# Attention inside a decoder layer: the chain that makes the shift rows two places later on VectorE and ScalarE, the rows' DMAs six places behind the group's last product

## What is computed

```python
q = (x @ Wq.T + bq).reshape(B, N, HEADS, HEAD_DIM).transpose(0, 2, 1, 3)
k = (context @ Wk.T + bk).reshape(B, M, HEADS, HEAD_DIM).transpose(0, 2, 1, 3)
v = (context @ Wv.T + bv).reshape(B, M, HEADS, HEAD_DIM).transpose(0, 2, 1, 3)
attn = jax.nn.softmax(jnp.einsum('bhnd,bhmd->bhnm', q, k) * scale, axis=-1)
out = jnp.einsum('bhnm,bhmd->bhnd', attn, v)
```

## Time and profile before

| what | value |
| --- | --- |
| median of 3 runs | 1926.51 us (1926.38 to 1927.36) |
| the profiled execution, its own time | 1935.45 us |
| its span in the trace | 1933.5 us |
| mean granted clock of TensorE | 0.971 |
| PE busy | 1824.7 us, 94% |
| DVE busy | 1430.8 us, 74% |
| ACT busy | 1251.9 us, 65% |
| POOL busy | 445.2 us, 23% |

### The profile page before, as it was taken

One profiled execution on the slowest core, in us unless ns is written; L12 is line 12 of the kernel. 1 busy time (PEld: TensorE's weight loads), 2 busy tenths in 40 slices (PEclk: granted clock), 3 DMA queues, 4 the chain that ended last, 5 costly groups with the idle time before them and its releaser, 6 DMA issues. The chain is left out here.

```text
span 1933.5 us, 38723 instructions
## 1 busy us (share of the span) xinstructions
PE 1824.7 (94%) x12524; PEld 1288.2 (67%) x12524; DVE 1430.8 (74%) x3030; ACT 1251.9 (65%) x3128; POOL 445.2 (23%) x629
## 2 busy tenths in 40 slices
PE   7899999999999999789999999989999999899988
PEld 5677777777777777564666666656666663588853
DVE  8988888888888888647686868667777775566348
ACT  5646464646464645348989898878888886266614
POOL 1312121212121212421222121222232222100006
PEclk9999999999999999898999999989999996799999
DMA  7122131313131313433334343334343423721266
GB/s 235 53 55 96 50 101 49 102 48 103 50 102 48 103 47 104 137 97 93 105 90 122 91 117 102 111 106 116 100 121 92 125 68 103 228 92 47 75 210 257
DMA packets 123884, 200.60 MB, mean 104 GB/s; under 512 B 27184, under 2 KB 48688, under 8 KB 123440
## 3 DMA queue, kind: packets, MB, share of 16 engines
q1 hardware_dynamic: 114480, 179.20, 30.1%
q0 software_dynamic: 9216, 18.89, 3.9%
HBM read 117.27 MB, written 29.88 MB: 76 GB/s over the span
## 5 line engine op out<-in xcount | busy, mean ns | idle before, releaser
L1961 ACT ACTIVATE a_shared<-a_shared,a_mx 128x512 f32<-128x512 f32 x512 | 344.4, 676 | 57.7 <-DVE a_mx L2024 57.5
L2024 DVE TENSOR_REDUCE a_mx<-a_shared 128x1 f32<-128x512 f32 x512 | 328.3, 682 | 37.9 <-PE a_shared L2171 36.2
L1954 ACT ACTIVATE a_probs<-a_scores 128x512 f32<-128x512 f32 x512 | 302.8, 607 | 58.8 <-PE a_scores L2182 58.6
L2171 PE MATMUL a_shared<-a_ks,a_qs 96*128 96x512 f32 x512 | 213.7, 438 | 13.8 <-ACT a_shared L1961 8.5
L2182 PE MATMUL a_scores<-a_qs,a_ks 98*128 98x512 f32 x512 | 211.3, 427 | 9.8 <-DMA a_qs<-a_shift_rows 5.2
L2143 PE MATMUL a_shared<-link 128*128 128x512 f32 x768 | 201.7, 399 | 9.7 <-DVE a_v L2018 7.4
L1086 PE MATMUL m_proj<-m_xt_hi,link 128*128 128x512 f32 x448 | 182.2, 407 | 3.9 <-DVE m_acc L780 3.5
L2171 PEld LDWEIGHTS a_shared<-a_ks,a_qs 96*128 96x128 f32 x512 | 96.2, 194 | 132.9 <-ACT a_shared L1961 59.5
L600 ACT ACTIVATE m_xw<-m_added,m_wdt 128x64 f32<-128x64 f32 x256 | 55.8, 329 | 192.7 <-DVE m_xdt L868 192.7
L2143 PEld LDWEIGHTS a_shared<-link 128*128 128x128 f32 x768 | 146.6, 192 | 47.3 <-DVE a_v L2018 10.9
L1087 PE MATMUL m_proj<-m_xt_lo,link 128*128 128x512 f32 x448 | 176.5, 394 | 0.0
(11 more groups left out here) (305 smaller groups left out, 3828.2 us busy)
## 6 DMA issues: line engine op xcount, KB each, us to landing
m_dec<-step_decay SPq DMA_DIRECT2D x64, 256.0 KB, 4.1
a_qs<-link SPq DMA_DIRECT2D x256, 64.0 KB, 2.0
m_ce<-run_decay SPq DMA_DIRECT2D x128, 112.0 KB, 3.1
a_ks<-a_k_hi POOLq DMA_DIRECT2D x192, 64.0 KB, 2.4
e_x<-x SPq DMA_DIRECT2D x11, 1024.0 KB, 5.6
m_xt_in<-x_t_in SPq DMA_DIRECT2D x8, 1024.0 KB, 9.6
m_x_tok<-x_in SPq DMA_DIRECT2D x8, 1024.0 KB, 5.4
x<-m_x_tok SPq DMA_DIRECT2D x32, 256.0 KB, 2.8
```

What stands on the lines that cost most here:

```text
L1954: act.activation(probs[:, n % 2, h, :], scores[t.score_bank(n, h)][:, :], ACT.Exp, scale=-1.0).then_inc(exp_ready, 1)
L1961: act.activation(scored[:, :], scored[:, :], ACT.Exp, scale=-1.0, bias=mx[:, i % 2, j, h:h + 1], accum_out=den[:, i, j, h:h + 1]).then_inc ...
L2024: dve.tensor_reduce(mx[:, i % 2, j, h:h + 1], bank(what)[:, :], AX.X, ALU.min).then_inc(mx_ready, 1)
L2171: pe.matmul(bank(what)[:, :], qs[0:STACK, t.slot(i), h, j * P:(j + 1) * P], ks[0:STACK, t.slot(i), h, :], start=True, stop=True).then_inc( ...
```

## The change

The chain starts two places later: `range` at lag 3, `log` at 4, `split` at 5, and SP's rows' DMAs are a step of their own, `rows`, at lag 6. Held-back sums are no longer put in at once behind the group's last maximum, but when `range` itself is put in. PE's order stays as it was.

```diff
-RANGE_LAG, LOG_LAG, SPLIT_LAG = 1, 2, 3
+RANGE_LAG, LOG_LAG, SPLIT_LAG, ROWS_LAG = 3, 4, 5, 6
...
             ending.extend([[lag, what, group, d] for lag, what in
-                           ((RANGE_LAG, "range"), (LOG_LAG, "log"), (SPLIT_LAG, "split"))])
+                           ((RANGE_LAG, "range"), (LOG_LAG, "log"), (SPLIT_LAG, "split"), (ROWS_LAG, "rows"))])
...
     def ended():
         for entry in list(ending):
             entry[0] -= 1
-            if entry[1] == "range":
+            if entry[0] == 0 and entry[1] == "range":
                 totals(0)
...
-                elif kind == "split":
+                elif kind == "rows":
                     sp.wait_ge(rows_ready, t.at(KT, i + 1))
```

## The result

The changed kernel takes **2010.45 us** (median of 4 runs, 2006.09 to 2014.23) against 1926.55 (4 runs, 1926.38 to 1927.36): a ratio of 1.0434, 95% interval 1.0413 to 1.0455, slower. The prediction was 1992 (1970 to 2022). The profiled execution took 2014.23 us, its span is 2012.2 (before: 1935.45 and 1933.5), its mean clock 0.955 (before: 0.971).

The account below looks back on a forecast made before the run. PE, busy 94% of the span, was taken to bound the kernel. Stalls of +47 us and clock falls of +18 made +65, from the profiled 1935.45 to about 2000, as a median 1992 us (+3.4%), range 1970 to 2022.

Parts of the forecast that it names:

- the forecast's own mechanism: Late rows in groups 2, 3 and 0, most long waits followed by a short clock fall: 1980 to 2006 us, chance 0.61.
- Copy of v: Group 1: `range` no longer stands ahead of DVE's copy of v, so seven waits of PE go, -7.0 us.
- Group 2: Transposition 2.2 us later in steady sequences with no slack, so PE's first product waits 2.7 us: +17.1 us in all.
- Group 3: Transposition 2.6 us later less 0.4 slack, so PE waits 2.25 us in each of seven sequences: +15.8 us.
- Group 0: Transposition 1.8 us later less 0.7 slack, 1.1 us in seven sequences, 2.5 in the very first group: +10.3 us.
- Group 1: Slack of 3 us covers DVE; rows behind two context loads on SP and later x loads: +1 us, bounds 0 and 5.
- `fetch`: Last sequence, group 3: SP issues the expert stage's loads ahead of the rows, delaying the first product: +10 us, 9 to 27.
- Stalls: Sum of all predicted changes in PE's waits over the kernel, before any effect of the clock: +47 us.
- The clock: PE's clock falls behind three in four of some 15 new waits, 1.6 us each: +18 us, bounds 0 and 51.
- the faster one: Rival: DVE's stand is the real cost, without it DVE runs ahead and `split` comes no later: 1916 us, chance 0.04.
- The rival with long falls or a late `fetch`: Rows late, and 11 falls cost 3.4 us each or the last sequence costs 27: 2008 to 2030 us, chance 0.17.

Follow-up runs that it names:

- a1: The changed kernel with the last sequence's expert-stage loads put back behind group 3's rows' DMAs on SP: 1998.05 us, ratio 1.0359 to the kernel before.
- a3: The kernel before with all chains at lags 3, 4, 5 and rows at 5 on SP, expert-stage loads behind the rows: 1988.22 us, ratio 1.0323.
- c3: The kernel before with only group 1's rows' DMAs issued three places later on SP, at lag 6: 1944.09 us, ratio 1.0074.
- a2: The kernel before with only SP in the change's order, rows at lag 6, expert-stage loads ahead of them in the last sequence: 1957.96 us, ratio 1.015.
- c1: The kernel before with `range` and the held-back sums one place later in all groups, `split` and rows untouched: 1928.89 us, ratio 0.9999.

## Why the prediction held, and where it was off

The sum was built on the transposition in groups 2, 3 and 0 ending later against PE, and it did. The size came out too low: 2010.45 lies within 1970 to 2022, but above the 1980 to 2006 that the forecast's own mechanism gave. It was held by the part of the range that a rival with another mechanism had added, so that much is luck. Point by point:

- **Copy of v, -7.0:** -7.4.
- **Group 2, +17.1:** in six steady sequences the wait went from 0.5 to 3.0 (predicted 2.7), in the first to 0.99, in the last from 2.21 to 3.86: +17.8.
- **Group 3, +15.8:** seven waits of 2.4, +16.9.
- **Group 0, +10.3:** 0.37 in the first group and not 2.5, but 1.11 once and 1.6 five times, one nearly none: +9.6. Two errors cancel. The 1.1 was too low because I held every group to the 3.96 us of group 2 from transposition to product. Where the rows are waited for, that way measures 4.13 us in group 2, 4.24 in group 3 and 4.49 in group 0 (from the rows above, as 1522.18 less 1517.69), so the slack of groups 3 and 0 was 0.1 to 0.2 us and not 0.4 and 0.7.
- **Group 1, +1 with bounds 0 and 5: this step failed.** In the changed kernel's trace it is 2.4 us of waiting for rows in the first sequence and 4.3 us for x, 6.7 in all, and a1 less a3, which differ only in the rows' place on SP, is 7 us (0 to 14); on the kernel before it costs 14.3 (c3), more than in the late kernel. I saw that the loads of x start later on SP by 0.8 and took it as free; it was 2.6 against before (c3), and I had no row for what waits on them.
- **`fetch`, +10:** 12 to 14 by a1; the term was worked out as 8.9 (rows ready at 1643.7, wanted at 1634.85). In the trace the wait is 13.36, 11.9 above a1's 1.48. The rows were issued 9.0 us behind the transposition, as foreseen. Their own way then took 5.00 us (1711.40 to 1716.40) against 3.93 in group 2 before, 1.1 more; and PE stood ready 0.7 us behind the transposition, in a1 only 2.4 behind it, 1.7 more. The paragraph behind this list says where the 1.1 lie.
- Stalls: 17.8 + 16.9 + 9.6 + 2.4 + 13.4 = 60.1, the 60.0 of the waits row; less 7.4, plus 4.3 for x, makes 57.0 where I had 47. The idle time as a whole grew by 55.3.
- **The clock, +18:** PE is busy 23.4 us longer in all and 30.8 in the six steady sequences. The falls are more than forecast: 17 stretches at 0.50 of some 3 to 7 us each between 912 and 1640 us, where I expected ten, and they cost about 2 us each (30.8, and the 3.4 of the one fall that before has there, over 16 stretches). The 1.5 us of the sum does not follow from its row: 9 instructions in 3 us in place of 13 are 0.9 us lost; but that fall lasted 7 us (857 to 864), which by the same rate is 2.1.
- The forecast of the profile: 24 waits (about 25), 65 us (some 50), longest 13.4 (near 10), the stand of DVE 2.5 (under 10), no wait for the copy of v. Of the rivals, the faster one is refuted by a3: DVE's stand vanished and `split` came later all the same. The rival with long falls or a late `fetch` (2008 to 2030) holds the measured time, and not its mechanism: the falls cost 2 us and not 3.4, `fetch` 12 to 14 and not 27.

In the last sequence, did the rows have to wait until the loads ahead of them had landed? The packets show it. Four rows' DMAs are 136 packets (before, from the issue to the product), and in a2, whose last sequence is alike (issued at 1656.67, product at 1660.77), the second line ends with the last of the rows' 128-byte packets:

```profile
DMA packets 136, 0.02 MB, mean 4 GB/s; under 512 B 136, under 2 KB 136, under 8 KB 136
DMA packets 460, 0.18 MB, mean 162 GB/s; under 512 B 150, under 2 KB 460, under 8 KB 460
DMA packets 25, 0.01 MB, mean 17 GB/s; under 512 B 5, under 2 KB 25, under 8 KB 25
```

(windows 1411.02 to 1414.95 of before, 1659.10 to 1660.18 and 1660.18 to 1660.77 of a2). Behind the rows' last packet 20 of the loads' 512-byte packets were still moving, and the last semaphore update of the loads came at 1661.09, when PE had already started. So the rows did not wait for the loads' landing. By the Trainium skill ("DMA: Bandwidth & Descriptors", queues, rings and completion order) completion is not first-in-first-out per issuing engine; this trace agrees. The rows' first packet did move later with the loads ahead of it, 2.4 us behind the first issue against 1.3 in the idle queue before (1412.33), but the last one came as soon, 3.5 us (before and a2) and 3.6 (the change, 1715.00) behind it. The 1.1 us lie behind that packet: from it to the product are 0.45 us before, 0.60 in a2 and 1.40 with the change, and what takes them is open.

78.7 us between the profiled executions stand against 83.9 between the medians, since before's profiled run lay 9 us above its median and after's 4.

What remains open: the last stretch of the rows' way with the change (1.40 us against 0.60 in a2); why c1's exponentials come later; what the rows' place on SP costs in the late kernel (0 to 14 us); and why one wait is followed by a fall of the clock and the next, as long, is not.

## What to carry to other kernels

Before you move a step, ask of each engine *and each queue* it issues on which block of work it crosses, not by how many places it moves: one place, which in group 2 crosses a block of 3 us, cost 52 us over the four groups of eight sequences, the second place 10 more. Four tiny DMAs are 2.7 us of issue time, free where the queue idled, and where it was busy PE waited up to 1.65 us for the load behind them. And an engine's stand in the waits is no loss by itself: the 55.5 us of DVE vanished and the kernel became slower; the part that gained was the single place (group 1) where another engine's wait hung on it.

## What was not expected of the hardware

Waits of PE as short as 1.62 us are followed by a stretch at 1.2 GHz in some sequences and not in others. With the change, the product at 1522.18 had waited 1.62 us and the clock was 0.50 behind it; the one at 1633.22 had waited 1.58, the one at 1496.66 even 2.39, and behind these it stayed at 1.00. The same order of steps has a different number of falls from one execution to the next: a1 and the change have the same order in the steady sequences, and PE is busy 602.1 us there in the one and 610.6 in the other.

A fall need not end soon where PE is busy again. In the kernel before, behind the wait of 2.2 us at 1611.27 in the last sequence, the clock was 0.50 for some 50 us, though PE was busy 45 of the 47 us shown (columns as in the earlier trace rows):

```profile
1613.00:1660.00 47.00, 45.26 (x133) 18.02 (x133) 20.62 (x41) 29.02 (x69) 8.30 (x4) 0.50 0.66 198
```

c1 shows the same stretch (0.51 from 1606 to 1658). It is also why a mean clock of the whole kernel (0.971 and 0.955) says little of what the new waits cost.
